# Edge layer of a four-layer graph network: node rows spread in a PSUM bank, five homes for one-hots, keys turned a slot ahead, two engines written out

## Chip, cores and metric

One core of a Trainium2 chip. The metric is the device time of one execution in microseconds: 14562.36 us, the median of three runs (14559.02 to 14573.27).

## The reference

Four message-passing layers over 12500 nodes of 64 features and 400000 edges sorted by target (`dst`). Only the first, the edge layer, is touched. Cut to it:

```python
h = jnp.maximum(_layernorm(x, axis=-1), 0.0)
edge_features = jnp.concatenate([h[dst], h[src] - h[dst]], axis=-1)
m = jax.nn.relu(edge_features @ W1 + b1) @ W2 + b2
out = jax.ops.segment_max(m, dst, num_segments=12500)
x = x + jnp.where(jnp.isfinite(out), out, 0)
```

The kernel computes `A[dst] + B[src]` with tables A and B made once per node, then relu, the product with W2 and the running maximum. The layers behind it add neighbours' rows through matrices that count how often source q feeds target block b; these counts are made in the edge layer too.

## The kernel before

Each of the 128 partitions (lanes) owns 3125 consecutive edges. They are done in 125 **slots** of K = 25 edge columns; slot b uses ring place r = b % 5 of `ring` and `fill` (R = 5 places each), and five slots make one turn of a loop. What each engine does for a slot:

- **GpSimd** (`gather_slot` L612, `gather_keys` L624): 25 indirect DMAs, each fetching one row of B per lane (`ring`, L620), and one for the keys of the block (`crow`, L628). It waits only for the indices, which SyncE loads (`pass_index` L642) when slot b - 4 is scanned and slot b - 5 stored. GpSimd and SyncE run a `Fori` loop; GpSimd's work has no other wait.
- **VectorE** (`slot0` L1399, `scan_steps` L1352, `hist_batch` L1328, `count_batch` L1337, `open_slot` L1382):
  - ten **batches** of one-hots, two for a histogram and eight for the block's counts. A batch is two `tensor_tensor` comparisons in bf16 (`row_onehots`, L673): `ohq` of 16 x 128 elements, `ohr` of 16 x 98. There are two homes for batches in `HM`, so each waits until TensorE has used the batch before the last;
  - 25 **fill steps** (L1360): the row of A for each edge column, `fill[j] = keep[j] * fill[j-1] + fill[j]`, for slot b + 1;
  - 25 **max steps** (L1360): the running maximum `ring[j] = max(min(ring[j-1], mask[j]), om[j])`, for slot b, from the product in PSUM. Fill and max steps are chains: each step waits on a semaphore for the one before it. Between two comparisons there stand three steps in the order max, fill, max;
  - at the end (`open_slot`): wait for slot b + 1's rows, the key difference `ckey` (L1389), the sum of the 25 rows of `ring` and `fill` in one operation (L1391); then the copy of the lane's keys (L1402) and the masks (L1373 to L1375).
- **TensorE** (`body0` L1858): transposes of the keys (L1864, L1865) and of the summed rows (`turn`, L1854), the product with W2 (L1877), the histogram and, for each counts batch, four groups of eight matmuls into two banks `bk` (L1823), each waiting for ScalarE to empty the bank before the last.
- **ScalarE** (`slot0` L1704): copy of the turned keys (`kb`, L1708), relu of the turned rows (L1716), 32 evictions of counts to bytes (L1700), and the DMAs that store counts and edge rows.

The order is written by hand. The four quarters of a slot (8, 8, 8 and 1 columns) are stages: VectorE waits for a quarter's product (`products0`), builds two count batches with that quarter's max steps between, then signals `taken0`. The quarters are seen in the trace as **pairs** of batches.

VectorE's code is written out for the first and last turn (slots 0 to 4 and 120 to 124, `body0(0)` and `body0(ITERS - 1)`), and a `Fori` loop for the turns between (L1442). In a loop semaphore values come from registers, so that a wait there is register arithmetic and a `gate`, a semaphore increment that holds the wait (`wait` L295, `gate` L300):

```python
def wait(e, name, n):
    if not (isinstance(n, int) and n <= 0):
        e.wait_ge(sem(name), n)
def gate(e):
    e.sem_inc(sem("gate_" + e.engine.name), 1)
```

Behind the edge layer GpSimd reads the last row of each node (L898) and the next layers follow; they need the whole edge layer.

Of the kernel before, what the change touches and what calls it, by code (L numbers as in the profile page):

```python
# [28 lines left out]
VB = P // VS  # L29
CW = VB * 4  # L30
# [27 lines left out]
def build(nc, x, src, dst, edge_weight, l0_w1, l0_b1, l0_w2, l0_b2, l1_w, l1_b,  # L58
# [7 lines left out]
    with ctx:  # L66
# [63 lines left out]
        dupjunk = sb("dupjunk", [P, 2, 4, P], bf16)  # L130
# [19 lines left out]
        lane_keys = sb("lane_keys", [P, 2, K, 2], bf16)  # L150
# [52 lines left out]
        base, iota_p = kp[:, 0:TILES], kp[:, P:2 * P]  # L203
        bk = [ps(f"bk{k}", [P, 512]) for k in range(2)]
# [9 lines left out]
        def mm_banks(name, u):  # L214
# [20 lines left out]
        ohq = [h_half[:, u * P * VS:(u + 1) * P * VS].rearrange("p (k q) -> p k q", q=P) for u in range(2)]  # L235
        ohr = [h_half[:, 2 * P * VS + u * TILES * VS:2 * P * VS + (u + 1) * TILES * VS]
               .rearrange("p (k q) -> p k q", q=TILES) for u in range(2)]

        kb = eqw_words.bitcast(bf16)[:, 0:2 * 2 * P * 2].rearrange("p (u a k h) -> p u a k h", u=2, a=2, h=2)
        masks = dupjunk[:, :, :, :].rearrange("p a b c -> p (a b c)").bitcast(f32)[:, 0:R * 2 * K]\  # L240
            .rearrange("p (r a k) -> p r a k", r=R, a=2)
# [919 lines left out]
        def _(e):  # L1161
# [102 lines left out]
            def virtual_rows():  # L1264
# [32 lines left out]
                chain(e.tensor_scalar(node128, nodek, float(P), None, ALU.mult))  # L1297
# [7 lines left out]
                chain(e.tensor_copy(lastT[:, :], pb[:, 0:BLOCKS]))  # L1305

# [21 lines left out]
            def hist_batch(b, h):  # L1328
                wait(e, "banked", b * CW - (4 if h == 0 else 0))
                gate(e)  # L1330
                for oh, a, m in ((ohq, 0, P), (ohr, 1, TILES)):
                    last = row_onehots(e, oh[h], lane_keys[:, a, HIST[h].start:HIST[h].stop, :], m)
                    if a == 1:
                        last.then_inc(sem("batched"), 1)
                    yield

            def count_batch(b, r, v):  # L1337
                if v == 0:
                    wait(e, "keys_copied", b + 1)
                if v < 2:  # L1340
                    wait(e, "histed", b * 2 + (v + 1))
                else:
                    wait(e, "banked", b * CW + (v - 1) * 4)
                gate(e)
                for oh, a, m in ((ohq, 0, P), (ohr, 1, TILES)):
                    last = row_onehots(e, oh[v % 2], kb[:, r % 2, a, v * VS:(v + 1) * VS, :], m)
                    if a == 1:
                        last.then_inc(sem("batched"), 1)
                    yield


            def scan_steps(chain, buf, b, r, mask, op0, op1, cols, other=None):  # L1352
                for n, j in enumerate(cols):
                    prev = buf[:, r, j - 1, :] if j else buf[:, (r - 1) % R, K - 1, :]
                    if isinstance(b, int) and b + j == 0:
                        prev = zero_row[:, :]
                    this = buf[:, r, j, :] if other is None else other[:, n * D:(n + 1) * D]
                    if chain.n:
                        e.wait_ge(sem(chain.name), chain.n)
                    e.scalar_tensor_tensor(out=buf[:, r, j, :], in0=prev, scalar=mask[:, j:j + 1],  # L1360
                                           in1=this, op0=op0, op1=op1).then_inc(sem(chain.name), 1)
                    chain.n += 1
                    yield

            def settle(chain):
                e.wait_ge(sem(chain.name), chain.n)
                chain.clear()

            fill_chain, max_chain = Chain(e, "v_fill"), Chain(e, "v_max")

            def masks_of(b, r):
                chain = loop_chain
                chain(e.tensor_copy(masks[:, r, 0, :], keep[:, bass.ds(b * K, K)]))  # L1373
                chain(e.tensor_scalar(masks[:, r, 1, :], masks[:, r, 0, :], 2.0, -1.0, ALU.mult, ALU.add))
                chain(e.tensor_scalar(masks[:, r, 1, :], masks[:, r, 1, :], FULL, None, ALU.mult))  # L1375

            def fill_steps(b, r, i):
                wait(e, f"first{r}", i * 16 + 16)
                gate(e)
                return scan_steps(fill_chain, fill, b, r, masks[:, r, 0, :], ALU.mult, ALU.add, range(K))  # L1380

            def open_slot(b, r, i):  # L1382

                settle(fill_chain)
                e.sem_inc(sem("filled0"), 1)
                wait(e, f"moved{r}", i * (16 * (K + 1)) + 16 * (K + 1))
                wait(e, "keys_turned", b)
                gate(e)
                e.tensor_scalar(ckey[:, :], crow[:, r, 0:CH], node128T[:, bass.ds(b, 1)], None, ALU.subtract)\  # L1389
                    .then_inc(sem("keyed"), 1)  # L1390
                loop_chain(e.tensor_tensor(ring[:, r, :, :], ring[:, r, :, :], fill[:, r, :, :], ALU.add))  # L1391
                loop_chain.clear()
                e.sem_inc(sem("summed0"), 1)
# [5 lines left out]
            def slot0(b, r, i, nb, nr, ni):  # L1399
# [27 lines left out]
                if nb is not None:  # L1427
                    open_slot(nb, nr, ni)
# [532 lines left out]
```

## Time and profile before

| | |
|---|---|
| median of three runs | 14562.36 us |
| the profiled execution | 14569.2 us |
| its span, first to last instruction | 14567.5 us |
| mean granted TensorE clock | 0.707 |
| edge layer, slots | about 567 to 5281 us |
| VectorE busy, of the span | 9170.7 us (63%) |
| GpSimd busy | 7878.9 us (54%) |
| TensorE matmul busy | 7325.4 us (50%) |
| ScalarE busy | 5837.4 us (40%) |

DVE is VectorE, ACT ScalarE, PE TensorE, POOL GpSimd, SP SyncE. A group of instructions is given as line, engine, operation, output<-inputs and count, then its busy time and the mean ns of one, then the engine's idle time just before them with what ended it; "issue" is a wait for nothing that the profile shows. A row of a timeline has start and duration in us, then the same, with idle time and its releaser in brackets. The releaser is inferred from semaphores: where several are waited for, it is the one that came last by the profile. Semaphore, register and branch instructions do not count as busy.

### The profile page before, as it was taken

To read this page: it belongs to the slowest core of one execution; us is meant where nothing else is said; L and a number is where in the kernel's file an instruction comes from. 1 tells how busy PE (TensorE), PEld (TensorE's weight loads), DVE (VectorE), ACT (ScalarE), POOL (GpSimd) and SP (SyncE) were. 2 spreads that over 40 slices of the span, in tenths; PEclk is the share of its full clock that TensorE was granted. 3 is DMA by queue.
4 is the path that set the end of the run, shared out by engine and by line. 5 is a ranking of instruction groups with operands and counts; after the bars stand their busy time and mean duration, and the time that the engine had idled before them with its cause. 6 is when DMAs were issued, how large, how long until landed. Compare 5 with 4: busy or idle time off the path is not lost. (4 is left out here: it accounts for less than half of the span.)

```text
span 14567.5 us, 284975 instructions
## 1 busy us (share of the span) xinstructions
PE 7325.4 (50%) x96792; PEld 5293.3 (36%) x96792; DVE 9170.7 (63%) x18445; ACT 5837.4 (40%) x10200; POOL 7878.9 (54%) x7259
## 2 busy tenths in 40 slices
PE   2266666666666638995998899400000000000553
PEld 1255555555555524553555455300000000000553
DVE  5488888888888883335334333566666566665672
ACT  0144444444444426773775577222222222222000
POOL 5677777777777741110111111477777777777002
PEclk9866666666666659997998999555555555555775
DMA  7333333333333328665764866222222222221782
GB/s 312 128 108 117 117 108 117 109 116 117 108 117 117 108 77 315 196 195 204 226 196 143 305 196 196 82 65 64 64 65 66 62 64 67 64 64 50 249 255 79
DMA packets 1257578, 1969.44 MB, mean 135 GB/s; under 512 B 246673, under 2 KB 975868, under 8 KB 1251775
## 3 DMA queue, kind: packets, MB, share of 16 engines
q1 hardware_dynamic: 854751, 1046.51, 23.6%
q10 hardware_dynamic: 168176, 611.00, 10.7%
q0 software_dynamic: 233744, 299.93, 7.7%
q8 instruction: 558, 9.14, 0.3%
q14 instruction: 349, 2.86, 0.1%
HBM read 1155.02 MB, written 815.51 MB: 135 GB/s over the span
## 5 line engine op out<-in xcount | busy, mean ns | idle before, releaser
L620 POOL DMA_INDIRECT RF<-tab_edge_b,idx x3125 | 3549.3, 1136 | 1035.9 <-issue 947.2
L1147 POOL DMA_INDIRECT records<-RF,idx x3125 | 3145.3, 1006 | 984.3 <-issue 984.3
L673 DVE TENSOR_TENSOR HM<-iota_b,eqw 128x2048 bf16<-128x2048 bf16 x2000 | 2201.6, 1101 | 352.8 <-PE bk L1823 198.1
L1700 ACT ACTIVATE X<-bk 128x392 uint8<-128x392 f32 x4000 | 1792.4, 495 | 1556.3 <-PE bk L1823 1534.3
L864 POOL DMA_INDIRECT agg<-RF,lastT x372 | 518.5, 1394 | 3222.8 <-ACT RF L806 3132.0
L1823 PE MATMUL bk<-HM 128*64 128x98 bf16 x32000 | 1587.8, 247 | 1304.2 <-ACT X L1700 670.1
L1823 PE MATMUL kp<-HM,ident_b 128*64 128x98 bf16 x6250 | 281.6, 283 | 3778.7 <-DVEq L1605 3778.7
L764 PE MATMUL tp<-HM,RF 128*64 128x512 bf16 x12276 | 2122.0, 384 | 96.5 <-ACT HM L716 69.0
L1823 PEld LDWEIGHTS bk<-HM 128*64 128x64 bf16 x32000 | 1240.8, 134 | 1654.4 <-issue 1569.8
L1823 PEld LDWEIGHTS kp<-HM,ident_b 128*64 128x64 bf16 x6250 | 261.5, 168 | 3799.7 <-issue 3799.7
L770 PE MATMUL om<-HM,RF 128*64 128x512 bf16 x6138 | 1424.9, 383 | 0.0
L764 PE MATMUL tp<-RF 128*64 128x512 bf16 x5952 | 1091.8, 386 | 254.4 <-ACT RF L716 232.2
L764 PEld LDWEIGHTS tp<-HM,RF 128*64 128x64 bf16 x12276 | 924.7, 110 | 737.0 <-issue 185.8
L1360 DVE SCALAR_TENSOR_TENSOR RF<-RF,dupjunk 128x64 f32<-128x64 f32 x3124 | 866.4, 277 | 27.3
L1360 DVE SCALAR_TENSOR_TENSOR RF<-RF,dupjunk,om 128x64 f32<-128x64 f32 x3124 | 842.0, 270 | 0.4
L1761 ACT ACTIVATE RF<-qblk 128x50 f32<-128x50 f32 x125 | 31.8, 254 | 1976.4 <-DMA records<-RF,idx 1941.6
L716 ACT ACTIVATE RF<-dst_f 128x4096 bf16<-128x4096 uint8 x186 | 672.8, 3617 | 355.9 <-PE tp L764 235.1
L716 ACT ACTIVATE HM<-dst_f 128x4096 bf16<-128x4096 uint8 (+1 forms) x186 | 703.5, 3823 | 137.5 <-DMA dst_f<-counts 89.4
L718 DVE CAST HM<-dst_f 128x4096 bf16<-128x4096 uint8 x186 | 427.0, 2296 | 501.6 <-PE tp L764 204.4
L770 PE MATMUL om<-RF 128*64 128x512 bf16 x2976 | 736.9, 385 | 0.0
L716 ACT ACTIVATE HM<-crow 128x4096 bf16<-128x4096 uint8 x186 | 671.6, 3611 | 53.0 <-DMA crow<-counts 44.0
L764 PEld LDWEIGHTS tp<-RF 128*64 128x64 bf16 x5952 | 492.9, 111 | 522.8 <-issue 283.7
(362 smaller groups left out, 15307.5 us busy)
## 6 DMA issues: line engine op xcount, KB each, us to landing
dst_f<-counts SPq DMA_DIRECT2D x465, 512.0 KB, 3.8
RF<-first_rows SPq DMA_DIRECT2D x250, 800.0 KB
counts<-X ACTq DMA_DIRECT2D x250, 784.0 KB
RF<-records SPq DMA_DIRECT2D x220, 784.0 KB, 4.5
crow<-counts SPq DMA_DIRECT2D x279, 512.0 KB
records<-RF ACTq DMA_DIRECT2D x2, 57680.0 KB, 214.4
first_rows<-RF ACTq DMA_DIRECT2D x25, 4000.0 KB
edge_rows<-RF ACTq DMA_DIRECT2D x125, 800.0 KB
```

Source lines behind the costliest of these rows:

```text
L620: e.indirect_dma_start(out=ring[:, r, j, :], out_offset=None, in_=table[:, :], in_offset=bass.IndirectOffsetOnAxis(ap=idx[:, r, j:j + 1], ...
L673: return e.tensor_tensor(to[:, 0:n, :].rearrange("p k (q h) -> p k q h", h=2), iota_b[:, 0:m].rearrange("p (q h) -> p q h", h=2).unsqueeze ...
L716: e.activation(to, of, ACT.Copy).then_inc(sem("widened_A"), 1)
L718: e.tensor_copy(to, of).then_inc(sem("widened_D"), 1)
L764: last = e.matmul(tp[u][k * D:(k + 1) * D, :], hi_mid[:, t, k * D:(k + 1) * D], part, start=t == 0, stop=t == TILES - 1, skip_group_check= ...
L770: return e.matmul(om[u][k * D:(k + 1) * D, :], low[:, t, :], part, start=t < 2, stop=t >= TILES - 2, skip_group_check=True)
L864: e.indirect_dma_start(out=agg[:, :], out_offset=bass.IndirectOffsetOnAxis(ap=lastT[:, g * GB + k:g * GB + k + 1], axis=0), in_=out_rows[g ...
L1147: e.indirect_dma_start(out=records[:, :], out_offset=bass.IndirectOffsetOnAxis(ap=idx2[:, r, j:j + 1], axis=0), in_=msgs[MSG_OF[r]][:, j, ...
L1360: e.scalar_tensor_tensor(out=buf[:, r, j, :], in0=prev, scalar=mask[:, j:j + 1], in1=this, op0=op0, op1=op1).then_inc(sem(chain.name), 1)
L1700: e.activation(staged[u].rearrange("p (r k) -> p r k", k=P)[:, :, k:k + 4], bk[s % 2][:, 0:4 * TILES].rearrange("p (k r) -> p r k", k=4), ...
L1761: e.activation(msgs[MSG_OF[r]][:, :, RW - 2:RW], qblk[:, r, :].unsqueeze(2).broadcast_to([P, K, 2]), ACT.Copy)
L1823: last = e.matmul(to[k:k + D, :], by_q[:, k:k + D], by_r, start=start, stop=stop, skip_group_check=True)
```

## The change

Five parts, all in the edge layer:

1. **Fill steps into PSUM.** The filled row of column j goes to `spread(j)`, column block j % 8 of the bank `kp`, instead of back to `fill`. After columns 7, 15, 23 and 24 one `tensor_tensor` adds the bank to those ring columns. The first of these waits for slot b + 1's gathers (`moved`), in the third batch of slot b; `open_slot` goes.
2. **Five homes** for batches (`BATCHES = 5`), in all of `HM`; the waits for a free home move accordingly.
3. **Masks once for all slots**: `keepL` (tail of `HM`) is made ahead of the layer; the steps read `keep` and `keepL` by column, `masks_of` goes.
4. **Keys a slot ahead**: key difference (an activation with bias, `node128` negated) and key copy go to ScalarE (`slot_keys`, in quarter 1 of slot b for b + 1, waiting for `moved`); TensorE turns them ahead of quarter 3 into a free part of `tp[1]`, ScalarE copies them in quarter 3 (`copy_keys`).
5. **Written out**: VectorE's and ScalarE's code has no loop any more, waits have constants and no gates. TensorE's, GpSimd's and SyncE's loops stay.

```diff
+        turned_keys = tp[1][:, 2 * P:4 * P]
+        spread = lambda j: kp[:, j % 8 * D:(j % 8 + 1) * D]
...
+            def batch(b, k):
+                if k < BATCHES:
+                    wait(e, "banked", (b - 1) * CW + (k + BATCHES - 1) * 4)
+                elif k < BATCHES + 2:
+                    wait(e, "histed", b * 2 + (k - BATCHES + 1))
+                else:
+                    wait(e, "banked", b * CW + (k - BATCHES - 1) * 4)
+                if k == 2:
+                    e.wait_ge(sem("keys_copied"), b + 1)
...
+            def fill_steps(b):
+                r, i = b % R, b // R
+                e.wait_ge(sem(f"first{r}"), i * 16 + 16)
+                for j in range(K):
+                    prev = zero_row[:, :] if b + j == 0 else spread(j - 1) if j else spread(K - 1)
+                    last_of(fill_chain)
+                    link(fill_chain, e.scalar_tensor_tensor(out=spread(j), in0=prev, scalar=keep[:, b * K + j:b * K + j + 1],
+                                                            in1=fill[:, r, j, :], op0=ALU.mult, op1=ALU.add))
                     yield
...
+                    if j % 8 == 7 or j == K - 1:
+                        if j == 7:
+                            e.wait_ge(sem(f"moved{r}"), (i + 1) * 16 * (K + 1))
+                        rows = ring[:, r, j // 8 * 8:j + 1, :]
+                        last_of(fill_chain)
+                        link(fill_chain, e.tensor_tensor(rows, rows, kp[:, 0:(j % 8 + 1) * D].rearrange("p (k f) -> p k f", f=D),
+                                                         ALU.add))
+                        yield
+                last_of(fill_chain)
+                e.sem_inc(sem("filled0"), 1)
+                e.sem_inc(sem("summed0"), 1)
...
+            def slot0(b):
+                filling = fill_steps(b + 1) if b + 1 < BLOCKS else iter(())
+                e.wait_ge(sem("keyed"), b + 1)
+                for k in range(3):
+                    for _ in batch(b, k):
                         several(filling, 2)
                 for q, cols in enumerate(MAXQ):
...
+                    e.wait_ge(sem("products0"), b * NQ + q + 1)
+                    taking = max_steps(b, q)
                     for v in range(2 * q + 1, min(2 * q + 3, VB)):
+                        for _ in batch(b, v + 2):
                             several(taking, 1)
                             several(filling, 1)
                             several(taking, 1)
                     several(taking, len(cols))
...
+            def slot_keys(b):
+                r = b % R
+                e.wait_ge(sem(f"moved{r}"), (b // R + 1) * 16 * (K + 1))
+                wait(e, "keys_turned", b)
+                e.activation(lane_keys[:, b % 2, :, :, :], qr[:, :, b * K:(b + 1) * K].unsqueeze(3)
+                             .broadcast_to([P, 2, K, 2]), ACT.Copy)
+                e.activation(ckey[:, :], crow[:, r, 0:CH], ACT.Identity, bias=node128T[:, b:b + 1])\
+                    .then_inc(sem("keyed"), 1)
...
+                        if q + 1 == 1:
+                            wait(e, "keys_copied", b + 1)
+                            gate(e)
+                        if q + 1 == NQ - 1:
+                            wait(e, "copied0", b * NQ + (NQ - 2))
+                            gate(e)
+                            if not (isinstance(i, int) and b == BLOCKS - 1):
+                                turn_keys(b + 1, (r + 1) % R)
```

## Rows read from the trace of the kernel before

**Rows 1.** Busy time in one stretch, then granted clock, DMA share, GB/s.

```profile
2548.00:2912.00 364.00, 225.45 (x3784) 189.75 (x3784) 316.92 (x730) 162.29 (x359) 283.19 (x251) 0.68 0.35 108
```

**Rows 2.** Groups of instructions in the loop, 1092 to 4732 us.

```profile
L620 POOL DMA_INDIRECT RF<-tab_edge_b,idx x2410 | 2732.3, 1134 | 771.2 <-issue 730.5 <-DMA cix<-chunk_lin 40.6
L673 DVE TENSOR_TENSOR HM<-iota_b,eqw 128x2048 bf16<-128x2048 bf16 (+1 forms) x1536 | 1691.8, 1101 | 260.6 <-PE bk L1823 156.6 <-PE mixed L1823 75.5 <-PE om L1877 21.2
...
L1823 PE MATMUL bk<-HM 128*64 128x98 bf16 x24581 | 1219.7, 247 | 1009.7 <-ACT X L1700 515.6 <-DVE HM L673 477.2 <-issue 6.0
...
L1391 DVE TENSOR_TENSOR RF<-RF 128x1600 f32<-128x1600 f32 x96 | 173.9, 1812 | 0.0
```

**Rows 3.** Timeline of VectorE in the loop: start us, us.

```profile
2514.66 1.28 DVE L673 TENSOR_TENSOR HM<-iota_b,eqw 128x2048 bf16<-128x2048 bf16 x1 [0.52 <-PE bk L1823]
...
2517.91 1.21 DVE L673 TENSOR_TENSOR HM<-iota_b,eqw 128x2048 bf16<-128x2048 bf16 x1
...
2519.62 0.96 DVE L673 TENSOR_TENSOR HM<-iota_b,eqw 128x1568 bf16<-128x1568 bf16 x1
...
2521.68 1.28 DVE L673 TENSOR_TENSOR HM<-iota_b,eqw 128x2048 bf16<-128x2048 bf16 x1 [0.52 <-PE bk L1823]
...
2534.83 1.22 DVE L673 TENSOR_TENSOR HM<-iota_b,lane_keys 128x2048 bf16<-128x2048 bf16 x1 [0.37 <-DVE dupjunk L1375]
...
2567.32 0.30 DVE L1389 TENSOR_SCALAR ckey<-crow,node128T 128x128 f32<-128x128 f32 x1
...
2570.96 1.23 DVE L673 TENSOR_TENSOR HM<-iota_b,lane_keys 128x2048 bf16<-128x2048 bf16 x1 [0.37 <-DVE dupjunk L1375]
```

**Rows 4.** Timeline of GpSimd in the loop, same stretch.

```profile
2514.68 0.94 POOL L620 DMA_INDIRECT RF<-tab_edge_b,idx  x1 [0.30 <-issue]
...
2518.52 1.41 POOL L620 DMA_INDIRECT RF<-tab_edge_b,idx  x1 [0.30 <-issue]
2520.24 1.16 POOL L620 DMA_INDIRECT RF<-tab_edge_b,idx  x1 [0.30 <-issue]
2521.71 0.94 POOL L620 DMA_INDIRECT RF<-tab_edge_b,idx  x1 [0.30 <-issue]
```

**Rows 5.** Timeline of VectorE in a written-out slot.

```profile
5161.06 1.23 DVE L673 TENSOR_TENSOR HM<-iota_b,eqw 128x2048 bf16<-128x2048 bf16 x1 [0.37 <-PE bk L1823]
...
5165.96 0.97 DVE L673 TENSOR_TENSOR HM<-iota_b,eqw 128x1568 bf16<-128x1568 bf16 x1
...
5167.88 1.22 DVE L673 TENSOR_TENSOR HM<-iota_b,eqw 128x2048 bf16<-128x2048 bf16 x1 [0.37 <-PE bk L1823]
```

**Rows 6.** Timeline of GpSimd beside that written-out slot.

```profile
5161.24 1.86 POOL L620 DMA_INDIRECT RF<-tab_edge_b,idx  x1 [0.30 <-issue]
5163.41 1.16 POOL L620 DMA_INDIRECT RF<-tab_edge_b,idx  x1 [0.30 <-issue]
5164.87 1.41 POOL L620 DMA_INDIRECT RF<-tab_edge_b,idx  x1 [0.30 <-issue]
...
5168.05 1.87 POOL L620 DMA_INDIRECT RF<-tab_edge_b,idx  x1 [0.30 <-issue]
```

**Rows 7.** Groups of GpSimd beside written-out slots, 5104 to 5186 us.

```profile
L620 POOL DMA_INDIRECT RF<-tab_edge_b,idx x51 | 64.4, 1262 | 15.5 <-issue 15.5
```

**Rows 8.** Timeline of VectorE where its loop branches back.

```profile
2647.76 0.21 DVE L1402 COPY lane_keys<-dst_f 128x100 bf16 x1 [5.37 <-issue]
```

**Rows 9.** Groups of VectorE in the last layer: rows in PSUM.

```profile
L1587 DVE SCALAR_TENSOR_TENSOR tp<-tp,mblk,RF 128x64 f32<-128x64 f32 x1740 | 509.1, 293 | 97.1 <-DVE tp L1587 27.2
...
L1614 DVE TENSOR_TENSOR bk<-bk,RF 128x512 f32<-128x512 f32 x232 | 154.4, 693 | 146.5 <-ACT RF L1770 146.5
```

**Rows 10.** Timelines of GpSimd and VectorE at the ends of the layer.

```profile
642.43 0.94 POOL L620 DMA_INDIRECT RF<-tab_edge_b,idx  x1 [12.64 <-DMA cix<-chunk_lin]
...
5185.65 0.94 POOL L628 DMA_INDIRECT crow<-kr,cix  x1 [0.30 <-issue]
...
5281.19 0.54 DVE L1445 MEMSET RF<- 128x576 f32 x1
```

More of the change, by code:

```diff
@@ L1296, in virtual_rows @@
                 e.sem_inc(sem("rows_vector"), 1)
[L1297 removed]
+                chain(e.tensor_scalar(node128, nodek, -float(P), None, ALU.mult))
                 chain(e.tensor_scalar(tgtk, nodek, -SKIP, None, ALU.add))
@@ L1335, in hist_batch @@
                     yield
[L1337 to L1348, printed above, removed]
-                    yield
@@ L1352, in scan_steps @@
[L1352 to L1362, printed above, removed]
-                    yield
@@ L1365, in settle @@
[L1365 to L1393, printed above, removed]
+            fill_chain, max_chain = Chain(e, "v_fill"), Chain(e, "v_max")
@@ new lines, in max_steps @@
+            def max_steps(b, q):
+                r = b % R
+                for n, j in enumerate(MAXQ[q]):
+                    prev = zero_row[:, :] if b + j == 0 else ring[:, r, j - 1, :] if j else ring[:, (r - 1) % R, K - 1, :]
+                    last_of(max_chain)
+                    link(max_chain, e.scalar_tensor_tensor(out=ring[:, r, j, :], in0=prev, scalar=keepL[:, b * K + j:b * K + j + 1],
+                                                           in1=om[q % 2][:, n * D:(n + 1) * D], op0=ALU.min, op1=ALU.max))
+                    yield
@@ L1421, in slot0 @@
                     several(taking, len(cols))
-                    e.wait_ge(sem(max_chain.name), max_chain.n)
+                    last_of(max_chain)
                     e.sem_inc(sem("taken0"), 1)
-                settle(max_chain)
                 e.sem_inc(sem("scanned"), 1)
-                several(filling, K)
-                if nb is not None:
-                    open_slot(nb, nr, ni)
-            def body0(i):
-                for r in range(R):
-                    b = i * R + r
-                    if isinstance(i, int) and i == ITERS - 1 and r == R - 1:
-                        slot0(b, r, i, None, None, None)
-                    else:
-                        slot0(b, r, i, b + 1, (r + 1) % R, i + (r + 1) // R)
-            e.wait_ge(sem("tab0"), 16 * NGROUPS)
-            masks_of(0, 0)
-            several(fill_steps(0, 0, 0), K)
-            open_slot(0, 0, 0)
-            body0(0)
-            with e.Fori(1, ITERS - 1) as i:
-                body0(i)
-            body0(ITERS - 1)
+                several(filling, K + NQ + 1)
+            e.wait_ge(sem("tab0"), 16 * NGROUPS)
+            chain(e.tensor_scalar(keepL, keep[:, :], 2.0, -1.0, ALU.mult, ALU.add))
+            chain(e.tensor_scalar(keepL, keepL, FULL, None, ALU.mult))
+            several(fill_steps(0), K + NQ + 1)
+            for b in range(BLOCKS):
+                slot0(b)
+            e.wait_ge(sem("histed"), 2 * BLOCKS)
+            e.wait_ge(sem("banked"), CW * BLOCKS)
             chain(e.memset(zero_tile, 0.0))
@@ L1856, in turn, with turn_keys @@
                 last.then_inc(sem("turned0"), 1)
+            def turn_keys(b, r):
+                wait(e, "keyed", b + 1)
+                gate(e)
+                e.transpose(turned_keys[:, 0:P], ckey[:, :], ident[:, :])
+                e.transpose(turned_keys[:, P:2 * P], crow[:, r, CH:2 * CH], ident[:, :]).then_inc(sem("keys_turned"), 1)
             def body0(i):
@@ L1883, in body0 @@
                         block_counts(b, v)
-            loop(e, body0)
+            turn_keys(0, 0)
+            body0(0)
+            with e.Fori(1, ITERS - 1) as i:
+                body0(i)
+            body0(ITERS - 1)
             fix_tensor(e, 0)
```

105 lines of the change are left out of this document (47 added, 58 removed).

## Prediction

> **What bounds the kernel now.** Read the busy time by stretch first: in one stretch of the edge layer VectorE is busy 317 of 364 us, GpSimd 283, ScalarE 162 and TensorE 225 at a granted clock of 0.68 [rows 1]. Neither of the first two looks full. The groups over ten such stretches tell more. GpSimd's gathers take 1.134 us each, with 730.5 us of "issue" before 2410 of them (0.303 each); a slot has 26, so 26 x 1.437 = 37.4 us [rows 2]. Beyond that GpSimd waits only 40.6 us, for indices. The stretch of 3640 us holds 2410/25 = 96.4 slots, 37.8 us each: GpSimd has work for all but 0.4 us of a slot. VectorE's slot is 36.13 us (first one-hot to first one-hot), and once in five slots its loop branches back with 5.37 us idle [rows 3, 8]: 37.2 us. So both engines stand within 2% of the bound, and the question is what each does to the other.
>
> The two timelines side by side show that. Take a pair of batches, one-hots A, B, C, D and A again. C runs from 2517.91 to 2519.12; a gather starts at 2518.52, inside it, lasts 1.41 and ends at 2519.93, 0.81 after C. D ends at 2520.58; the gather begun inside it ends at 2521.40, 0.82 after D [rows 3, 4]. A gather that starts outside a one-hot takes 0.94. So a gather begun while a two-input SBUF operation runs cannot proceed until that ends, and then needs 0.82. The next starts 0.30 later: 1.12 after D's end. In the loop A starts 1.10 after D's end, and the gather at 2521.71 is 0.03 behind it, still free at 0.94 (as is that at 2514.68, 0.02 behind): GpSimd does **five gathers per pair** of 7.02 us. It is a near miss of 0.02 to 0.03 us.
>
> Slots 0 to 4 and 120 to 124 are already written out in this kernel: no register arithmetic, A after 0.37 us of idle time and not 0.52, though the trace names the same TensorE wait; so that idle time is sequencer time. There D ends at 5166.93, A starts at 5167.88 (0.95 later), the gather at 5168.05 is 0.17 inside A and takes 1.87 (1.22 - 0.17 + 0.82): **four gathers per pair** of 6.82 us [rows 5, 6]. Over 5104 to 5186 us a gather averages 1.262 and a slot 26 x (1.262 + 0.304) = 40.7 us [rows 7]. A shorter VectorE pair gives a slower GpSimd.
>
> **The change, part by part.**
> Written-out VectorE: the branch goes (5.37 us in five slots), and so does the register arithmetic. Without the gates, one sequencer instruction fewer than in rows 5 stands between pairs. Two fewer made 0.52 into 0.37, so one is worth about 0.1: idle 0.27, pair 6.72, and A starts 0.85 after D. It must be over 1.08 for five gathers.
> Opening of a slot: from 2567.32 to 2570.96 VectorE spends 3.64 us on key difference, 1600-element add, key copy and masks [rows 3]; all leave it or are split. In their place come three adds of 512 and one of 64 with an input in PSUM: 0.69 each for the former [rows 9], 0.2 taken for the latter, with waits on the fill chain 2.6 us together. Two increments behind the chain cost 0.6 (between 0.3 and 0.8, from the idle times 0.37 and 0.52).
> Fill steps into PSUM: 293 ns against 277 busy in rows of the same form [rows 9]; between other work nothing to 0.02 each, 0 to 0.5 us a slot, 0 taken.
> Five homes: they save VectorE's wait on the histogram, 75.5 us, and perhaps the 21.2 on products: 0.9 us a slot [rows 2]. The 156.6 us booked to TensorE's banks is the sequencer time above, and homes save none of it.
> VectorE's work in a slot: 36.13 - 3.64 + 2.6 + 0.6 - 3 x 0.25 - 0.9 = **34.0 us**, between 33 and 35.5.
> Keys turned a slot ahead, copies on ScalarE: three small activations for two moved off VectorE, on an engine busy 162 of 364 us [rows 1]; nothing. TensorE has the same matmuls and waits 477 us for one-hots in 96 slots [rows 2], 5 us each; nothing, unless TensorE needs over 34 us. Behind the new wait of ScalarE for the next slot's rows stand its evictions, and behind those TensorE; but VectorE waits for the same rows in its third batch, so all resume together. GpSimd's and SyncE's instructions are unchanged.
> The new wait: VectorE needs slot b+1's rows about 5 us into slot b, where before it needed them at its end. As GpSimd is the slower, VectorE waits there in each slot once it has caught up, and meanwhile gathers run free, at 0.94 + 0.30 = 1.24.
>
> **The slot after.** While VectorE works (34.0 us), gathers go at 1.566 as in the written-out slots: 21.7 of them. The other 4.3 run free: 5.3 us. Slot 39.3. With four gathers per pair of 6.72 throughout (1.68 each): 20.2, then 5.8 free, 41.2. With the loop's 1.437 throughout: 37.4. I take 39.6, near the first, since those rows are this arrangement; a little above, since the pair is 0.1 shorter.
> The layer: GpSimd is first held by the ring at 642.43, until slot 1 is scanned [rows 10]; with slots 0 and 1 shorter by some 3 us each, 635. Then 120 slots x 39.6 = 4752: 5387. Landing 2 (0 to 5, no row shows it). VectorE then has the rest of its slot (34.0 - 5) and the last one, 30 without fill: 5448. Before, it ended at 5281.19, 95 us behind the last gather at 5185.65 [rows 10]. So **+167 us**. What follows starts when the layer ends and shifts with it. The profiled execution took 14569.2 us (span 14567.5), 7 above the median 14562.36: 14736 against its own time, **14730** against the median.
>
> The SBUF page of the Trainium skill ("SBUF — State Buffer", the section with the diagram of the two sides) says that GpSimd and a VectorE operation with two SBUF inputs take a shared port pair as an exclusive lock, whichever starts first holding it for its whole instruction. By that rule 26 gathers of 0.94 and nine pairs of one-hots of 1.22 and 0.96 could not overlap, and a slot would be over 44 us. The trace agrees for gathers behind one-hots and differs the other way: a one-hot beginning 0.02 to 0.03 before a gather is only 0.06 longer [rows 3, 4], so the measurement decides.
>
> **The rivals.**
> (a) The forecast, slots of 38.5 to 40.8 us: +35 to +311. Chance 0.72.
> (b) Other side: GpSimd keeps its pace of 37.4. Place: the boundary of a pair. It decides if A comes 1.08 or more after D, by PSUM steps longer than taken, or a wait for products, together 0.23 us a pair; or if the mix of pairs with adds falls as well. Then 635 + 4488 + 61 = 5184: -97, 14465. For it: one add makes one of three pairs longer than 7.0. Against: it needs all three. 0.12.
> (c) Every pair locks at four and the slot is 41.2: 635 + 4944 + 61 = 5640, +359, 14921. 0.06.
> (d) The change doesn't do that: effects cancel. Break-even slot (5281 - 61 - 635)/120 = 38.2. 0.07.
> (e) VectorE sets the end, gathers being hardly held: slot 0 begins two slots (75 us) before 642, so 567 + 125 x 34.0 = 4817, -464, 14098. The free pace of 26 x 1.24 = 32.2 allows it; rows 7 speak against it. 0.03. The Runtime page of the Trainium skill ("Instruction fetch mechanics") says a taken branch outside the fetched window stalls, and prefers unrolling. The trace agrees on the stall, 5.37 us [rows 8]; its advice holds where VectorE is the bound, as here only (e) has it.
>
> **The numbers.** Predicted is (a)'s 14730. The range leaves out (b), (e) and part of (c): 14540 to 14900, about 0.8. Some 0.2% (29 us) is what a measurement of this kernel can tell from no change. Faster: (b) + (e) = 0.15; within: (d) 0.07; slower: (a) + (c) = 0.78.
>
> **What would show it.** Right: gathers' mean rises from 1.134 to 1.22, with 1.1, 1.4, 1.1, 1.8 in turn; no index waits on GpSimd; pairs of 6.7 us; some 5 us of idle time on VectorE before the first 512-element add of each slot; layer end near 5450. Wrong: a mean at or under 1.13, pairs over 7.0, or VectorE idle elsewhere than at that add, as where TensorE became late.

## The result, and the profile of the changed kernel

The changed kernel takes **14703.53 us** (median of 4 runs, 14700.32 to 14706.62) against 14563.32 (4 runs, 14559.02 to 14573.27): ratio 1.0095, 95% interval 1.0079 to 1.0111. That is 140 us slower; forecast were 167 slower. The profiled execution took 14703.66 us (span 14701.9).

The same stretch as [rows 1], busy times of TensorE, its weight loads, VectorE, ScalarE and GpSimd, then granted clock, DMA share and GB/s:

```profile
2548.00:2912.00 364.00, 224.97 (x3691) 189.04 (x3689) 300.10 (x691) 161.30 (x368) 290.56 (x242) 0.69 0.33 107
```

VectorE is busy 17 us less than before, GpSimd 7 us more. Yet GpSimd begins 242 instructions there against 251: each of them is longer, which the busy time alone would hide. The groups over 1092 to 4732 us, which answer to [rows 2], and the largest waits of VectorE and TensorE in that stretch:

```profile
L624 POOL DMA_INDIRECT RF<-tab_edge_b,idx x2318 | 2814.8, 1214 | 706.4 <-issue 706.4
L677 DVE TENSOR_TENSOR HM<-iota_b,eqw 128x2048 bf16<-128x2048 bf16 x1484 | 1624.1, 1094 | 123.7 <-PE om L1881 61.6 <-DVE RF L1389 42.5 <-PE bk L1815 19.4
L1377 DVE TENSOR_TENSOR RF<-RF,kp 128x512 f32<-128x512 f32 (+1 forms) x371 | 211.0, 569 | 471.8 <-DMA crow<-kr,cix 465.3
...
DVE RF L1377 <- DMA crow<-kr,cix: 465.3, 91, 6.3
...
PE bk L1815 <- DVE HM L677: 787.0, 429, 6.6
```

A gather takes 1.214 us in place of 1.134, and the 40.6 us of waits for indices are gone: GpSimd never stops. There are 2318/25 = 92.7 slots in the 3640 us, 39.3 us each, against 37.8. VectorE waits 465.3/91 = 5.1 us in each slot ahead of the first add of the next slot's rows. Its one-hots hardly wait for a home any more, but TensorE now waits 787 us for them in place of 477. TensorE waits for VectorE's data, and VectorE for GpSimd's.

The two timelines side by side, first VectorE's one-hots and that add, then GpSimd's gathers. They answer to [rows 3, 4]; the fused short operations between the one-hots are left out:

```profile
2501.90 0.69 DVE L1377 TENSOR_TENSOR RF<-RF,kp 128x512 f32<-128x512 f32 x1 [5.97 <-DMA crow<-kr,cix]
...
2520.28 1.23 DVE L677 TENSOR_TENSOR HM<-iota_b,eqw 128x2048 bf16<-128x2048 bf16 x1 [0.21 <-PE bk L1815]
...
2522.00 0.97 DVE L677 TENSOR_TENSOR HM<-iota_b,eqw 128x1568 bf16<-128x1568 bf16 x1
...
2523.46 1.22 DVE L677 TENSOR_TENSOR HM<-iota_b,eqw 128x2048 bf16<-128x2048 bf16 x1
...
2525.17 0.97 DVE L677 TENSOR_TENSOR HM<-iota_b,eqw 128x1568 bf16<-128x1568 bf16 x1
...
2526.93 1.22 DVE L677 TENSOR_TENSOR HM<-iota_b,eqw 128x2048 bf16<-128x2048 bf16 x1 [0.21 <-DVE RF L1389]
```

```profile
2498.29 0.95 POOL L632 DMA_INDIRECT crow<-kr,cix  x1 [0.30 <-issue]
...
2520.62 1.71 POOL L624 DMA_INDIRECT RF<-tab_edge_b,idx  x1 [0.30 <-issue]
2522.63 1.16 POOL L624 DMA_INDIRECT RF<-tab_edge_b,idx  x1 [0.30 <-issue]
2524.09 1.41 POOL L624 DMA_INDIRECT RF<-tab_edge_b,idx  x1 [0.30 <-issue]
2525.80 1.16 POOL L624 DMA_INDIRECT RF<-tab_edge_b,idx  x1 [0.30 <-issue]
2527.26 1.71 POOL L624 DMA_INDIRECT RF<-tab_edge_b,idx  x1 [0.30 <-issue]
```

Call the one-hots from 2520.28 on A, B, C and D. Each of the four gathers that begin between 2520.28 and 2526.93 meets one of them and ends 0.82 us after it: 2522.33 after A's 2521.51, 2523.79 after B's 2522.97, 2525.50 after C's 2524.68, 2526.96 after D's 2526.14. The next gather begins at 2527.26, 1.12 us after D. A began 0.79 us after D and is 0.33 under way. So VectorE's pair of batches takes 6.65 us (2526.93 - 2520.28), less than the 7.02 before, and holds **four gathers in place of five**.

Two things in the timelines of 1092 to 4732 us complete this. The second pair of each slot also contains a 512-element add and takes 7.04 to 7.06 us, longer than the 7.02 of before, and it holds four gathers all the same: what counts is not the pair's length but how long after D the next A begins. And in the kernel before not every pair has five: the first pair of a slot has four in 89 of 96 slots, the second has five or six in all, the third five in 77.

The ends, which answer to [rows 10]: GpSimd's restart behind the ring's first turn, its last gather, and VectorE's end of the layer.

```profile
640.58 1.57 POOL L624 DMA_INDIRECT RF<-tab_edge_b,idx  x1 [4.16 <-DMA cix<-chunk_lin]
...
5366.88 0.95 POOL L632 DMA_INDIRECT crow<-kr,cix  x1 [0.30 <-issue]
...
5430.81 0.54 DVE L1426 MEMSET RF<- 128x576 f32 x1 [2.70 <-PE bk L1815]
```

The layer ends at 5430.81 against 5281.19: +149.6 us. The rest of the kernel takes 9272.9 us against 9288.0, 15 us less. The scatter of the records is what differs there, 3129.8 us for 3125 instructions against 3145.3; the change doesn't touch it, and I leave those 15 us unexplained.

### The profile page after: what moved, and what is told of

Read it like the earlier page. It is cut to its first block and busy times, and to the rows that moved or that the text cites. A ratio compares the mean times of both kernels' runs of the same rounds, so it can differ in the third digit from the quotient of the medians.

```text
span 14701.9 us, 272794 instructions
## 1 busy us (share of the span) xinstructions
PE 7383.9 (50%) x96792; PEld 5320.5 (36%) x96792; DVE 9080.9 (62%) x18197; ACT 5895.4 (40%) x10450; POOL 8093.9 (55%) x7259
## 5 line engine op out<-in xcount | busy, mean ns | idle before, releaser
L624 POOL DMA_INDIRECT RF<-tab_edge_b,idx x3125 | 3788.8, 1212 | 985.3 <-issue 951.1
L1151 POOL DMA_INDIRECT records<-RF,idx x3125 | 3129.8, 1002 | 984.4 <-issue 984.4
L1369 DVE SCALAR_TENSOR_TENSOR kp<-kp,keep,RF 128x64 f32<-128x64 f32 x3124 | 900.9, 288 | 31.8
L1389 DVE SCALAR_TENSOR_TENSOR RF<-RF,HM,om 128x64 f32<-128x64 f32 x3124 | 855.3, 274 | 0.4
```

The source lines that it names most:

```text
L624: e.indirect_dma_start(out=ring[:, r, j, :], out_offset=None, in_=table[:, :], in_offset=bass.IndirectOffsetOnAxis(ap=idx[:, r, j:j + 1], ...
L1151: e.indirect_dma_start(out=records[:, :], out_offset=bass.IndirectOffsetOnAxis(ap=idx2[:, r, j:j + 1], axis=0), in_=msgs[MSG_OF[r]][:, j, ...
L1369: link(fill_chain, e.scalar_tensor_tensor(out=spread(j), in0=prev, scalar=keep[:, b * K + j:b * K + j + 1], in1=fill[:, r, j, :], op0=ALU. ...
L1389: link(max_chain, e.scalar_tensor_tensor(out=ring[:, r, j, :], in0=prev, scalar=keepL[:, b * K + j:b * K + j + 1], in1=om[q % 2][:, n * D: ...
```

## The experiments

The theory: what counts is where the gathers of GpSimd fall against the one-hots of VectorE. The changed kernel is slower because the first one-hot of a pair now begins before the gather that follows the last one-hot. The rivals: the written-out code is itself slow; the new early wait for the next slot's rows takes the lead away; GpSimd is slowed by how much VectorE moves, not by when; or VectorE's work simply bounds the slot.

The runs fell on five chips, which make two groups. On three of them (e5 and e6; e7 to e9; e12) the kernel before took 14568 to 14577 us, about as in the runs that the prediction was made from. On the other two (e1 to e4; e10 and e11) it took 19414 and 19237 us. I take the edits in turn, and the other chips at the end.

### Two, three and four empty increments a quarter (e5, e7, e6)

```diff
                     e.sem_inc(sem("taken0"), 1)
+                    if q < NQ - 1:
+                        for _ in range(2):
+                            gate(e)
```

The range is 2 in e5, 3 in e7, 4 in e6. They stand behind each of the first three quarters. An increment of a semaphore that nobody waits for moves no data, and costs VectorE's queue about 0.1 us: the idle time ahead of a pair is 0.21 us in the changed kernel and 0.41, 0.51 and 0.60 with two, three and four. Two:

> The same edit as in e1: two empty semaphore increments on VectorE's queue after each quarter's published result, about 0.1 us each, so that VectorE's pair of batches takes 6.84 us in place of 6.65 and its first one-hot begins about 1.0 us after the last one's end in place of 0.8. Meant for a chip on which the kernel before takes about 14560 us, as in the runs the prediction was made from. Lock theory: the gather that follows the last one-hot is free 1.12 us after it, so it still meets the next one-hot; four gathers in 6.84 us instead of in 6.65, each slot about 0.9 us longer, 14800 us (14750 to 14860), slower than the changed kernel's 14703. Rival, VectorE's work is not the bound and the rest is a lost lead: within 20 us of 14703. If this chip again needs 19400 us for the kernel before, TensorE's starved queue bounds the slots there and the run says nothing of either: 19250.

Measured: 14765.66 us (14760.82 to 14775.55), ratio to before 1.0138 (1.0121 to 1.0155). Four:

> The same edit as in e2: four such increments, the pair takes 7.03 us and the first one-hot begins about 1.2 us after the last one's end, past the 1.12 us at which the next gather has got in. Lock theory: five gathers for each pair of 7.03 us (1.41 each) in place of four in 6.65 (1.66 each), GpSimd's slot falls from 39.3 to 36.5-37 us although VectorE does more, and the kernel is faster than both: 14390 us (14300 to 14500). Rival, the time went to VectorE's extra waits or to the written-out code: 0 to 60 us slower than 14703, since four pads a quarter add 0.4 us to a pair. If this chip again needs 19400 us for the kernel before: 19300, and it says nothing of either.

Measured: **14457.31 us** (14454.66 to 14458.54), ratio 0.9925 (0.9909 to 0.9942): more work on VectorE, and faster than both kernels. Three:

> Three increments in place of e6's four, the changed kernel otherwise. The pair takes 6.94 us and its first one-hot begins 1.08 to 1.10 us after the last one's end, as in the loop of the kernel before, where the following gather got in. Lock theory with the threshold where the kernel before has it: the jump from four gathers per pair to five lies between two pads (14766) and three, and the run is at 14400 to 14480 us. With the threshold above 1.10 the pair keeps four gathers and the run is slower than two pads, at 14800 to 14850. Rival without a lock, in which pads only shift work: between the two neighbours, about 14610.

Measured: 14494.47 us (14491.78 to 14503.42), ratio 0.9951 (0.9935 to 0.9968), 14 us over the span that was given. The last one-hot of a pair and the first of the next in VectorE's timeline, with two increments:

```profile
2583.00 0.96 DVE L677 TENSOR_TENSOR HM<-iota_b,eqw 128x1568 bf16<-128x1568 bf16 x1
2584.95 1.23 DVE L677 TENSOR_TENSOR HM<-iota_b,eqw 128x2048 bf16<-128x2048 bf16 x1 [0.41 <-PE bk L1818]
...
2591.79 1.23 DVE L677 TENSOR_TENSOR HM<-iota_b,eqw 128x2048 bf16<-128x2048 bf16 x1 [0.41 <-DVE RF L1389]
```

with three, where VectorE's rows are followed by GpSimd's gather at the same place:

```profile
2585.73 0.97 DVE L677 TENSOR_TENSOR HM<-iota_b,eqw 128x1568 bf16<-128x1568 bf16 x1
2587.78 1.29 DVE L677 TENSOR_TENSOR HM<-iota_b,eqw 128x2048 bf16<-128x2048 bf16 x1 [0.51 <-PE bk L1818]
...
2587.82 0.94 POOL L624 DMA_INDIRECT RF<-tab_edge_b,idx  x1 [0.30 <-issue]
```

with four, in the same way:

```profile
2526.59 0.96 DVE L677 TENSOR_TENSOR HM<-iota_b,eqw 128x1568 bf16<-128x1568 bf16 x1
2528.72 1.22 DVE L677 TENSOR_TENSOR HM<-iota_b,eqw 128x2048 bf16<-128x2048 bf16 x1 [0.60 <-PE bk L1818]
...
2528.67 0.94 POOL L624 DMA_INDIRECT RF<-tab_edge_b,idx  x1 [0.30 <-issue]
```

Take A's start less D's end at the boundary. Two increments: 2584.95 - 2583.96 = 0.99 us; the pair lasts 6.84 (2591.79 - 2584.95) and still has four gathers, and each slot pays for the longer pair. Three: 2587.78 - 2586.70 = 1.08; the gather begins 0.04 inside the one-hot, is free (0.94 long), and the one-hot pays 0.06 (1.29 against 1.23). Four: 2528.72 - 2527.55 = 1.17; the gather is there first. The groups of the gathers over 1092 to 4732 us, for two, three and four increments in this order, each from its own kernel's trace:

```profile
L624 POOL DMA_INDIRECT RF<-tab_edge_b,idx x2286 | 2825.6, 1236 | 696.7 <-issue 696.7
```

```profile
L624 POOL DMA_INDIRECT RF<-tab_edge_b,idx x2436 | 2761.8, 1134 | 742.4 <-issue 742.4
```

```profile
L624 POOL DMA_INDIRECT RF<-tab_edge_b,idx x2455 | 2752.1, 1121 | 748.2 <-issue 747.6 <-DMA cix<-chunk_lin 0.6
```

The jump lies between 0.99 and 1.08 us, and three increments stand on its very edge. Of the gathers that begin within 0.05 us of the start of a 2048-element one-hot in e7's trace, 244 are free and began 0.033 to 0.045 us inside it; 39 are held, and they began 0.044 to 0.050 inside. In the kernel before, 275 are free and none of these began more than 0.044 inside. A held one takes 2.00 us in place of 0.94, so the 39 cost some 41 us in that stretch; that is about the 37 us by which e7 is slower than e6, although it executes less.

The jump goes against the work added: 0.2 us more costs 62 us, 0.1 more on top of it gives back 271. A rival in which increments only shift or add work has no place for that. It also shows that the new early wait is not the cause, since it stands in all of these.

### The kernel before, VectorE written out and nothing else (e9)

```diff
-            body0(0)
-            with e.Fori(1, ITERS - 1) as i:
+            for i in range(ITERS):
                 body0(i)
-            body0(ITERS - 1)
```

> The kernel before with VectorE's slots written out and nothing else, as in e4. Lock theory: in its written-out slots [rows 5, 6] the first one-hot begins 0.95 us after the last one's end and a pair of 6.82 us has four gathers, so all 125 slots take the 38.9 us of those, 1.1 us more than 37.8 in the loop, less the loop branches' 5.4 us once in five slots, which only count where GpSimd waits for indices (46.8 us in all, which go): 14620 to 14720 us, slower than before's 14565. Rival, the written-out code is a gain as it was meant to be, since the branches and the registers' arithmetic go: 14430 to 14540 us, and what made the change slower is in its other parts (the homes, the sums through PSUM, the keys).

Measured: 14833.28 us (14819.39 to 14837.21), ratio 1.0179 (1.0162 to 1.0196). That is 265 us slower than before, and 113 us beyond the span that was given. The sign decides for the theory; the size was missed because the span was worked out from slots of 38.9 us, although [rows 7] has 40.7 for slots of this kind, and e9's are 40.6 (3640 us for 2240/25 = 89.6 slots). VectorE's boundary of a pair, then GpSimd's gathers beside it, then their group:

```profile
2588.08 0.97 DVE L673 TENSOR_TENSOR HM<-iota_b,eqw 128x1568 bf16<-128x1568 bf16 x1
2590.00 1.23 DVE L673 TENSOR_TENSOR HM<-iota_b,eqw 128x2048 bf16<-128x2048 bf16 x1 [0.37 <-PE bk L1821]
```

```profile
2590.18 1.87 POOL L620 DMA_INDIRECT RF<-tab_edge_b,idx  x1 [0.30 <-issue]
2592.35 1.16 POOL L620 DMA_INDIRECT RF<-tab_edge_b,idx  x1 [0.30 <-issue]
2593.82 1.41 POOL L620 DMA_INDIRECT RF<-tab_edge_b,idx  x1 [0.31 <-issue]
2595.53 1.16 POOL L620 DMA_INDIRECT RF<-tab_edge_b,idx  x1 [0.30 <-issue]
```

```profile
L620 POOL DMA_INDIRECT RF<-tab_edge_b,idx x2240 | 2835.6, 1266 | 682.7 <-issue 682.7
```

A stands 0.95 us behind the last one-hot, and the four gathers are those of [rows 6], now in all slots; 1.266 us each is [rows 7] made the rule (1.262). So of the five parts of the change, the writing-out of VectorE brings more than the whole loss. The others together, the homes, the sums through PSUM, the masks, the keys and ScalarE's written-out code, give about 120 us of it back: 1.0179 - 1.0095 = 0.0084, give or take 0.0033, of 14568. I did not part them from one another. Whether two increments would bring e9 back, too, was tried in e11, on a slower chip only, and is open.

### Each one-hot in two halves (e8)

```diff
-                    last = row_onehots(e, oh[k % BATCHES], keys, m)
+                    half = (keys.shape[1] + 1) // 2
+                    row_onehots(e, oh[k % BATCHES], keys[:, 0:half, :], m)
+                    last = row_onehots(e, oh[k % BATCHES][:, half:, :], keys[:, half:, :], m)
```

> The same edit as in e3: each one-hot is written by two instructions of half its length, so a gather that meets one waits for the end of a half, 0.5 to 0.6 us, and not of a whole. VectorE pays about 0.07 us more for each one-hot (a pair 6.9 us). Lock theory: a gather's mean falls from 1.205 to about 1.05 us, GpSimd's slot to 35.3 us, where VectorE's own work is the bound, 14250 us (14150 to 14400), the fastest so far. Rival, gathers are slowed by VectorE's load on the memory and not by where its instructions begin and end: the same bytes are moved and the mean stays at 1.2 us, 14700 to 14760 us.

Measured: 14718.29 us (14707.9 to 14724.66), ratio 1.0102 (1.0085 to 1.0119). The number is the rival's, and the gathers' mean is 1.211 us. Neither theory nor rival had the rows right, though. Four of the gathers and, under them, one one-hot's two halves in VectorE's timeline (x2: two instructions in one row):

```profile
2564.24 1.18 POOL L624 DMA_INDIRECT RF<-tab_edge_b,idx  x1 [0.30 <-issue]
2565.73 1.36 POOL L624 DMA_INDIRECT RF<-tab_edge_b,idx  x1 [0.31 <-issue]
2567.40 1.94 POOL L624 DMA_INDIRECT RF<-tab_edge_b,idx  x1 [0.30 <-issue]
2569.64 1.22 POOL L624 DMA_INDIRECT RF<-tab_edge_b,idx  x1 [0.30 <-issue]
...
2567.22 1.29 DVE L677 TENSOR_TENSOR HM<-iota_b,eqw 128x1024 bf16<-128x1024 bf16 x2
```

The gather at 2567.40 begins in the first half and ends at 2569.34, 0.83 after the **second** one (2568.51): the place that the first half left free went to the second, not to the gather. Most get in between: of the gathers begun in a first half in the stretch of 1092 to 4732 us, 932 end 0.82 after that half and 143 after the second. I had assumed that all would. And halves back to back still leave four meetings in a pair of about 6.9 us: the lengths of these four, 1.18, 1.36, 1.94 and 1.22 us, with 0.30 behind each, make 6.9 in all. A load theory would have the same mean, but it has no answer to e6, e7 and e12, which move the same bytes as the changed kernel. What e8 takes away is my picture of the release, not the one of the phase.

### The same instructions in another order (e12)

```diff
+                    order = iter(("m", "mfm", "mfm", "mfmfm"))
                     for v in range(2 * q + 1, min(2 * q + 3, VB)):
                         for _ in batch(b, v + 2):
-                            several(taking, 1)
-                            several(filling, 1)
-                            several(taking, 1)
+                            for step in next(order):
+                                several(taking if step == "m" else filling, 1)
```

It ran first on one of the slower chips (e10), with this on record:

> Nothing is added or taken away: the twelve short operations between the four one-hots of a pair of batches stand 1, 3, 3, 5 in place of 3, 3, 3, 3, so that two of those that stood behind the first one-hot now lie ahead of the next pair's. VectorE's pair keeps its 6.65 us, but its first one-hot begins about 1.2 us after the last one's end in place of 0.8. Lock theory: five gathers get through a pair, and no time is paid for it: GpSimd's slot about 36 us, 14260 us (14200 to 14450), faster than the four pads' 14457. Rival, it was the pads themselves that helped (they hold back VectorE or publish its results sooner), not the place of the one-hots: the same work in another order stays within 40 us of 14703.

and then on one of the first group (e12):

> e10's kernel once more, for a chip on which the kernel before takes about 14565 us. Lock theory: 14260 us (14200 to 14450), faster than the four pads' 14457, GpSimd's slot at about 36 us with five gathers to each pair of about 6.65 us. Rival, the pads' gain was their own and not the place of the one-hots: within 40 us of 14703. On a chip that takes 19200 to 19400 us for the kernel before: 18920, as in e10.

Measured: **14331.97 us** (14329.2 to 14337.2), ratio 0.9833 (0.9817 to 0.9849), 245 us faster than before (14576.83 beside it) and some 370 us faster than the changed kernel. The boundary of a pair and the gathers' group:

```profile
2593.02 0.96 DVE L677 TENSOR_TENSOR HM<-iota_b,eqw 128x1568 bf16<-128x1568 bf16 x1
2595.16 1.22 DVE L677 TENSOR_TENSOR HM<-iota_b,eqw 128x2048 bf16<-128x2048 bf16 x1 [0.21 <-DVE RF L1389]
```

```profile
L624 POOL DMA_INDIRECT RF<-tab_edge_b,idx x2518 | 2729.7, 1084 | 767.6 <-issue 767.3 <-DMA cix<-chunk_lin 0.3
```

A now stands 1.18 us behind the last one-hot (2595.16 - 2593.98) although the idle time ahead of it is the 0.21 us of the changed kernel: two short operations moved there and no time was added. A gather takes 1.084 us. So it was the place of the one-hots and not the increments. This is the version to keep, and it has all five parts of the change.

Counted from the timelines of 1092 to 4732 us, over the three pairs of every slot (a few with missing records left out), gathers begun between one A and the next:

| kernel | A behind D, us | length of most pairs, us | pairs with 4, 5, 6 gathers |
|---|---|---|---|
| changed | 0.79 | 6.64, with an add 7.05 | 269, 7, 0 |
| e9 | 0.95 | 6.82 | 260, 7, 0 |
| e5, two increments | 0.99 | 6.84, with an add 7.25 | 261, 9, 0 |
| e7, three | 1.08 | 6.93 to 7.01, with an add 7.41 | 127, 158, 6 |
| before, loop | 1.10 | 7.02 | 108, 161, 19 |
| e6, four | 1.17 | 7.03, with an add 7.43 | 0, 294, 0 |
| e12, other order | 1.17 | 6.64, with an add 7.05 | 0, 303, 0 |

The changed kernel and e12 have pairs of the same length and the same instructions in them; only the distance from D to A differs.

### The other chips (e1 to e4, e10, e11)

There the kernel before took 19413.68 us beside e1 to e4 and 19236.65 beside e10 and e11, a third more. These were on record, for chips like those of the first group:

> The changed kernel with two semaphore increments more on VectorE between the pairs of batches (6 a slot, some 0.1 us each, no other work). Theory of the near miss: A starts about 0.99 after D's end, still under 1.08, so four gathers per pair, and the pair is 0.2 us longer: gathers' mean 1.22 to 1.25, slot 39.9 to 40.5, total 14780 (14740 to 14850), slower than the changed kernel's 14703. Rival, that the early wait for the next slot's rows is what costs: VectorE has 5 us of idle time in each slot there, so 0.6 us more work changes nothing, 14703 within 15.

> The same with four increments between pairs (12 a slot). Near miss: A starts about 1.2 after D's end, over 1.08, so the gather behind D is free and there are five gathers per pair of some 7.05 us: mean 1.10 to 1.14, slot 36.5 to 37.4, total 14400 (14340 to 14480), faster than both kernels although VectorE executes more. Rival of the early wait, and the rival that written-out code itself is slower: no change or slower, 14700 to 14760.

> The changed kernel with each one-hot comparison made as two of half the columns, back to back. Near miss, or rather the lock behind it: a gather waits for the end of the comparison it begins in, at most 0.6 us and not 1.1, so gathers' mean falls to 1.05 to 1.10 and GpSimd's slot under 36.5; VectorE's own slot grows from 34 to some 35.3 by 20 more fixed costs and becomes the bound. Total 14260 (14200 to 14380). Rival (early wait, or VectorE's density whatever its operations' length): gathers as slow as now, total 14703 or more.

> The kernel before with one edit: VectorE's loop over the turns of the edge layer is written out (constants, no register arithmetic, no branch); two homes, masks, the sum in SBUF, ScalarE and TensorE as before. Near miss: all slots look like its slots 120 to 124, pairs of 6.82, four gathers each: mean 1.22 to 1.26, slot 39.5 to 40.5, total 14720 (14650 to 14820), as slow as the changed kernel by this part alone. Rival, that the PSUM bank, the new wait or the keys' way cost: then this version is not slower than before; VectorE saves 5.4 us in five slots and GpSimd keeps 37.4: 14500 to 14563.

> e9's kernel, the kernel before with VectorE written out, and two empty increments after each quarter's published result. They take the pair from 6.82 to about 7.01 us and its first one-hot from 0.95 to 1.14 us behind the last one's end, where the loop of the kernel before had 1.10. Lock theory: what writing out had lost (14833 against 14568) comes back, GpSimd's slot falls from 40.6 to 37.8 us or a little under, 14480 us (14430 to 14580). Rival, the loss lay in the code itself, or in the gathers' wait having gone, and not in the phase: 14830 to 14900.

Measured, with the ratio to the kernel before on the same chip: e1 (two increments) 19256.49, 0.9921 (0.9904 to 0.9937); e2 (four) 19306.1, 0.9948 (0.9931 to 0.9965); e3 (halves) 19202.26, 0.9897 (0.988 to 0.9913); e4 (before, written out) 19359.87, 0.9973 (0.9962 to 0.9983); e10 (order) 18916.48, 0.9829 (0.9812 to 0.9845); e11 19256.87, 1.001 (1.0 to 1.002). None of these totals is near what was expected. The rows of e2 tell why: gathers and waits over 1092 to 4732 us, then TensorE, its weight loads, VectorE, ScalarE and GpSimd in two stretches of one slot.

```profile
L624 POOL DMA_INDIRECT RF<-tab_edge_b,idx x1383 | 1356.5, 981 | 2211.2 <-DMA cix<-chunk_lin 1806.4 <-issue 404.8
...
PE mixed L1818 <- issue: 1018.1, 1094, 4.9
...
2596.00:2608.00 12.00, 2.05 (x10) 1.07 (x10) 0.00 (x0) 0.00 (x0) 9.13 (x10) 0.50 0.12 27
2612.00:2616.00 4.00, 3.18 (x34) 2.95 (x34) 0.00 (x0) 0.60 (x1) 0.00 (x0) 0.52 0.00 0
```

While GpSimd gathers, TensorE issues 10 matmuls in 12 us, waiting for nothing that the profile shows; once GpSimd stops, 34 in 4 us. VectorE stands still in the first stretch: it waits for the product, 1584.8 us in the 3640. So a slot there is first GpSimd's 26 gathers and then VectorE's work, some 66 us in a row, and a gather that meets hardly any one-hot takes 0.981 us. That fits the theory (no one-hots, no long gathers) but doesn't test it, and what holds TensorE back is open. Against the first group, two increments, halves and the written-out VectorE have the other sign here; four increments and the order have the same. The order even has the same ratio, 0.9829 and 0.9833, although e10's gathers take 0.990 us and have next to nothing to gain. The changed kernel itself was not run on these chips, so what the order brings there, and by what, is not shown.

## Why the prediction was right

**The bound and the mechanism.** "Both engines stand within 2% of the bound", a gather that meets a one-hot ends 0.82 after it, and the next one-hot must begin 1.08 or more after D: the last two held, and in the first GpSimd was the bound, as taken. Forecast for the changed kernel were an idle time of 0.27 us, a pair of 6.72 and A 0.85 behind D; measured are 0.21, 6.65 and 0.79. Forecast lengths were 1.1, 1.4, 1.1, 1.8; measured are 1.16, 1.41, 1.16, 1.71. e5 and e7 put the threshold between 0.99 and 1.08, and e7, where 39 gathers of 283 are still held, puts it at 1.08. Two sentences of it were too wide. "Five gathers per pair", which the prediction read off one place, holds for the second and third pair of a slot of the kernel before, seldom for the first; the sum didn't suffer, since it used the mean of all gathers. And a gather is not held by every "two-input SBUF operation": of the fill steps of the kernel before, `scalar_tensor_tensor` of 64 elements with two SBUF inputs, none held a gather: 195 gathers began inside one, half of them with more than 0.13 us of it to come, and none took over 0.95 us. Comparisons and the 1600-element sum, all `tensor_tensor`, do hold it.

**The new wait.** "Some 5 us of idle time on VectorE before the first 512-element add": 465.3/91 = 5.1. "No index waits on GpSimd": none. TensorE waits longer for one-hots (787 us for 477), so it did not become the bound.

**VectorE's work in a slot**, 34.0: 39.3 - 5.1 = 34.2. That is a remainder and holds its other waits, too: those for the product were taken to shrink from 21.2 us in the stretch and grew to 61.6, 0.7 us a slot.

**The slot**, 39.6: from the first gather behind the ring's turn to the last, (5367.83 - 640.58)/120 = 39.39. This is the term that was too large, by 0.21 us, 25 us in 120 slots. I had gone a little above 39.3 because the pair is 0.1 shorter; the pace while VectorE works, 1.56 (34.2 us for the 26 - 5.1/1.24 = 21.9 gathers that are left), is that of the written-out slots, 1.566, and 39.3 would have been nearer. The three ways of working it out gave 37.4, 39.3 and 41.2; that the choice lay so close is more than they could promise, since 0.1 us in a slot is 12 us of the total.

**The start and the tail.** 635 was forecast for the first gather behind the ring, 640.58 came. VectorE's slots 0 and 1 became 1.4 and 5.7 us shorter, some 7 in all where 6 were taken. But slot 0 itself began 3.3 us later, and the gather began 1.9 us behind VectorE's slot 2, where before the two began together; neither was foreseen. The tail is 5430.81 - 5367.83 = 63.0 for 61. Landing took 2.66 and 2.97 us (2499.24 to 2501.90; 5367.83 to the add at 5370.80) for 2. Sum: -25 + 6 + 2 = -17, 5431 for 5448.

**Behind the layer** what follows was to start when the layer ends and shift with it; it became 15 us shorter, for a reason that is open. -17 and -15 are the 32 us between 14736 and 14703.66, so nearly half of the miss lies outside the layer.

**The rivals.** (b), GpSimd at its old pace, needed a boundary past the threshold; 1.08 - 0.79 = 0.29 us was lacking, where 0.23 had been said. That one add makes a pair longer than 7.0 spoke for it less than was thought: such pairs take 7.05 us and hold four. (e), VectorE sets the end, was far off in this kernel, where VectorE waits 5.1 us a slot for GpSimd. On the exclusive lock of the Trainium skill ("SBUF — State Buffer", the section with the diagram of the two sides): it says that whichever starts first has the ports for its whole instruction. The traces agree that a gather behind a one-hot is blocked, and differ in three places: a one-hot that starts 0.05 us after a gather is not held up at all (1.22, four increments), and of the 1797 of 2048 elements in e6 and e12, wherever in a gather they start, all but two take 1.23 us or less; a one-hot that starts 0.04 before a gather costs the gather nothing (0.94, three increments); and between two halves the second may go ahead of a waiting gather (e8).

## What to carry to other kernels

- Where GpSimd issues gathers one after another beside comparisons like these (`tensor_tensor`, two SBUF inputs, 0.96 and 1.22 us), a pair of batches holds four gathers or five, and which of them hangs on one distance. Work it out from the timeline, and how far it is from the threshold, before shortening or lengthening anything: here 0.2 us more was 0.4% slower, 0.4 us more 1.7% faster.
- Put the short operations together so that one gap is wide enough for a gather to begin in, rather than spreading them evenly: in another order the same instructions gave 2.5%.
- A change that shortens the work of an engine that isn't quite the bound may be a loss now and a gain after one more edit. Take its parts singly: writing VectorE out cost 265 us, the rest gave about 120 back.

## What the runs showed of the hardware beside that

The loop that left VectorE's code stays in TensorE's, and once in five slots TensorE stands still for nothing that the profile shows. With the phase mended, VectorE's wait behind it is its largest. In e12, TensorE's first transpose there and its first histogram product, and VectorE's one-hot ten us later:

```profile
2530.54 1.09 PE L1846 MATMUL tp<-ident,RF 128*128 128x128 f32 x4 [6.11 <-issue]
2535.60 0.29 PE L1815 MATMUL mixed<-HM 128*64 128x98 bf16 x2 [3.97 <-issue]
```

```profile
2541.23 1.23 DVE L677 TENSOR_TENSOR HM<-iota_b,eqw 128x2048 bf16<-128x2048 bf16 x1 [8.34 <-PE om L1881]
```

6.11 and 3.97 us of TensorE's, once in five slots, become 8.34 of VectorE's. That the branch of the loop is behind them is argued from their place alone. VectorE's other slots take some 34 us there and these 42, 35.6 in the mean, against GpSimd's 36.1: VectorE is all but the bound, as in rival (e). What writing TensorE out would bring was not tried.

The second thing is the other chips: the same programs, TensorE slowed to one matmul in 1.2 us while GpSimd issues gathers (e2), and with it another bound. A kernel tuned to the phase on one chip needs to be timed on more than one.
